# A feed-forward part that starts under the end of an attention part: the first norms of the last two batches, the second batch's bias step and the first activation are put in other places

## The reference, cut to what matters

```
x = x + attention(norm(x), ctx)          # 16 heads, softmax
x = x + ffn(norm(x))                     # the part of this change
x = x + mlstm(norm(x), ctx)              # 8 heads, gates, one junction over all batches
x = x + moe_lora(norm(x))

ffn:  h = layernorm(x) * ln1_g + ln1_b
      h = bitlinear(h, w1, b1)           # 256 -> 1024, activations rounded to 8 bits, weights ternary
      h = gelu(h)
      h = layernorm(h) * ln2_g + ln2_b
      h = bitlinear(h, w2, b2)           # 1024 -> 256
```

## Time and profile before

| | us |
|---|---|
| median of three runs | 413.37 |
| lowest, highest | 410.84, 414.47 |
| the profiled execution | 413.97 |
| its span in the profile | 412.3 |
| busy in the span: PE, DVE, ACT, POOL | 334.4, 305.8, 264.3, 183.8 |

### The profile page before, as it was taken

The page is one execution under the profiler, slowest core; times in us unless marked ns, Lnnn a source line. Parts: engine busy times, 40 slices in busy tenths (PEclk is TensorE's granted clock), DMA queues, the critical chain, the costliest instruction groups (busy, mean ns, idle before and its releaser), DMA issues.

```text
span 412.3 us, 9147 instructions
## 1 busy us (share of the span) xinstructions
PE 334.4 (81%) x3086; PEld 236.6 (57%) x3093; DVE 305.8 (74%) x1025; ACT 264.3 (64%) x567; POOL 183.8 (45%) x207
## 2 busy tenths in 40 slices
PE   2989789998999999724667778779488999999774
PEld 1777567776777767402445545456265666666431
DVE  2799736877889888676998999984447877788641
ACT  1466445476455455626789889876578888888520
POOL 1213401122122564239998989962015455544520
PEclk9999999999999999955999999989689999999966
DMA  7799998979634510000000000000002122212000
GB/s 239 211 291 264 262 249 221 234 177 227 134 85 115 123 22 2 1 0 0 2 1 2 0 2 1 2 0 2 0 14 40 40 41 53 52 46 46 16 25 25
DMA packets 43869, 33.68 MB, mean 82 GB/s; under 512 B 19888, under 2 KB 39728, under 8 KB 43696
## 3 DMA queue, kind: packets, MB, share of 16 engines
q1 hardware_dynamic: 43824, 33.11, 32.7%
HBM read 24.71 MB, written 8.39 MB: 80 GB/s over the span
## 4 chain that ended last, share of the span: by engine, by line
PE 57%; DVE 18%; issue 13%; ACT 8%; POOL 3%; DMA 1%; SPq 0%; DVEq 0%; ACTq 0%; POOLq 0%
PE PS L1461 6%; PE PS L1157 5%; PE PS L1238 5%; PE PS L1227 4%; DVE sm L741 4%; PE PS L1296 4%; PE PS L1218 4%; PE PS L1217 4%; PE PS L1451 4%; PE PS L1257 3%; PE PS L1446 3%; PE PS L1424 3%; ACT pT L991 2%; DVE sm L713 2%; PE PS L1400 2%
## 5 line engine op out<-in xcount | busy, mean ns | idle before, releaser
L991 ACT ACTIVATE pT<-PS 128x512 f32<-128x512 f32 x64 | 36.5, 596 | 48.2 <-PE PS L1218 47.9
L606 DVE TENSOR_REDUCE negm<-PS 128x4 bf16<-128x512 f32 x64 | 42.3, 684 | 13.0 <-PE PS L1227 12.8
L435 POOL TENSOR_TENSOR sm<-sm,mhalf 128x1 f32<-128x1 f32 x16 | 11.3, 708 | 81.1 <-DVE sm L638 81.1
L451 POOL TENSOR_TENSOR kst<-kst,rows 128x1024 f32<-128x1024 f32 x16 | 37.7, 2354 | 6.4 <-ACT kst L1059 6.3
L1103 ACT ACTIVATE lnT<-PS,Atok 128x128 f32<-128x128 f32 x128 | 36.5, 369 | 4.3 <-PE PS L1402 2.7
L1336 PE MATMUL PS<-identf,w2f 128*128 128x128 f32 x128 | 19.2, 298 | 21.0 <-ACT w2f L1048 20.8
L1218 PE MATMUL PS<-identb,negm 128*128 128x128 bf16 x256 | 34.9, 220 | 0.0
L465 POOL TENSOR_TENSOR kst<-kst,rows 128x1024 f32<-128x1024 f32 x14 | 33.1, 2366 | 0.0
L1238 PE MATMUL PS<-pT,vx 128*32 128x128 f32 x512 | 27.0, 285 | 5.2 <-ACT pT L991 5.2
L1336 PEld LDWEIGHTS PS<-identf,w2f 128*128 128x128 f32 x128 | 15.1, 151 | 25.5 <-ACT w2f L1048 20.2
L1461 PE MATMUL PS<-wd,xT 128*128 128x392 f32 x64 | 28.0, 565 | 1.8 <-DVE rest L885 1.8
(11 more groups left out here) (220 smaller groups left out, 975.6 us busy)
## 6 DMA issues: line engine op xcount, KB each, us to landing
scr_q<-qpart SPq DMA_DIRECT2D x8, 384.0 KB, 3.4
scr_k<-kpart SPq DMA_DIRECT2D x8, 384.0 KB, 4.5
X<-in_x SPq DMA_DIRECT2D x8, 256.0 KB, 4.6
CTXT<-in_ctxT SPq DMA_DIRECT2D x8, 256.0 KB, 4.8
vx<-in_ctx SPq DMA_DIRECT2D x16, 128.0 KB, 3.1
out<-rest SPq DMA_DIRECT2D x16, 128.0 KB, 1.7
rows<-in_rows SPq DMA_DIRECT2D x1, 1544.0 KB, 8.4
qst<-scr_q SPq DMA_DIRECT2D x8, 192.0 KB, 4.5
```

What stands on the lines that cost most here:

```text
L451: gp.tensor_tensor(n2[q.slot], n2[q.slot], ln2g, ALU.mult).then_inc(b_g2, 1)
L606: v.tensor_reduce(negm[f.slot % 2][:, 4 * hg:4 * hg + 4], PS[:, 2 + hg % 2, :].rearrange("p (h k) -> p h k", h=4), AX_X, ALU.max, negate=T ...
L991: s.activation(pT[:, hg, :], PS[:, hg % 2, :], ACT.Exp, scale=float(DH0) ** -0.5).then_inc(a_e, 1)
```

## The change

- GpSimd: the power (`spread1`) and the bias add (`residual`) of the first norm get functions of their own. For batch 14 the power stands inside turn 3, between the gain of batch 0 and the scale and shift, and the bias add behind turn 4; for batch 15 the power stands behind turn 4 and the bias add behind turn 6. Turn 2 comes ahead of them all.
- VectorE: the bias step of batch 1 stands ahead of the last residual update and of the first norm of batch 14, no longer in turn 2. Of batch 14, statistics and centring stand ahead of turn 2 and the scaling in turn 3, behind the bias step. Of batch 15, statistics and centring are in turn 4 and the scaling in turn 5. The two memsets of `mv23` stand ahead of the last `normalise`.
- ScalarE: the table set with gelu is asked for right behind the last exponential. In turn 2 the norm of batch 0 stands ahead of the gelu of batch 1. The roundings of batches 14 and 15 stand behind turns 4 and 6.
- TensorE: the transposes of batch 2 stand in the last attention turn, behind the transposes of batch 15's y.

```diff
--- before.py
+++ after.py
@@ -428,14 +428,19 @@
                 pool.wait_ge(s_wq, 3)
                 gp.tensor_scalar(row, row, by, None, ALU.mult).then_inc(s_sr, 1)
 
+            def spread1(d):
+                z = sm1[d.slot % 2]
+                pool.wait_ge(l_w, d.b + 1)
+                gp.tensor_tensor(z[:, 3:4], z[:, 2:3], mhalf[:, 0:1], ALU.pow).then_inc(l_r, 1)
+
+            def residual(d):
+                pool.wait_ge(l_c, d.b * 7 + 4)
+                gp.tensor_tensor(X[:, d.b, :], X[:, d.b, :], b2r, ALU.add).then_inc(l_xb, 1)
+
             def turn_a(_f, _b, _c, d):
                 if d:
-                    z = sm1[d.slot % 2]
-                    pool.wait_ge(l_w, d.b + 1)
-                    gp.tensor_tensor(z[:, 3:4], z[:, 2:3], mhalf[:, 0:1], ALU.pow).then_inc(l_r, 1)
-
-                    pool.wait_ge(l_c, d.b * 7 + 4)
-                    gp.tensor_tensor(X[:, d.b, :], X[:, d.b, :], b2r, ALU.add).then_inc(l_xb, 1)
+                    spread1(d)
+                    residual(d)
                     if 9 <= d.b < 12:
                         scale_rows(d.b - 9)
 
@@ -449,6 +454,9 @@
                         pool.wait_ge(s_sr, 3)
                     pool.wait_ge(b_n2, q.b + 1)
                     gp.tensor_tensor(n2[q.slot], n2[q.slot], ln2g, ALU.mult).then_inc(b_g2, 1)
+
+                if tau == 3:
+                    spread1(Turn(NB - 2, 2, 3))
                 if p or e:
                     now, was = tau % 2, (tau - 1) % 2
                     pool.wait_ge(b_ve, tau - 1)
@@ -465,11 +473,13 @@
                     gp.tensor_tensor(n2[q.slot], n2[q.slot], ln2b, ALU.add).then_inc(b_h2, 1)
 
             turn_a(*peeled(NB, NB, 4, 4))
-            turn_b(2, *peeled(2, NB, 4, 9))
-            turn_a(*peeled(NB + 1, NB, 4, 4))
-            turn_a(*peeled(NB + 2, NB, 4, 4))
-            for tau in range(3, NB + 8):
+            for tau in range(2, NB + 8):
                 turn_b(tau, *peeled(tau, NB, 4, 9))
+                if tau == 4:
+                    residual(Turn(NB - 2, 2, 3))
+                    spread1(Turn(NB - 1, 3, 3))
+                elif tau == 6:
+                    residual(Turn(NB - 1, 3, 3))
 
 
             def turn_cd(_n, _a, b, c, _e, _d):
@@ -752,8 +762,15 @@
                     biased(q)
                     if q.b == NB - 1:
                         scale2(q)
-                if b:
+                if b and b.b > 1:
                     hidden(b)
+
+                if tau == 3:
+                    ln1_scale(before_last, centred[0])
+                elif tau == 4:
+                    centred.append(ln1_centre(last, ln1_stats(last)))
+                elif tau == 5:
+                    ln1_scale(last, centred[1])
                 if d:
                     q4.start(d)
                     zd = sm4[d.slot % 2]
@@ -779,18 +796,16 @@
 
 
             first, last, before_last = Turn(0, 0, 0), Turn(NB - 1, 3, 3), Turn(NB - 2, 2, 3)
-            normalise(last)
             for i in range(2):
                 v.memset(mv23[i][:], 1.0).then_inc(b_mv, 1)
+            normalise(last)
             dve.wait_ge(b_mv, 2)
             stats2(first, 1)
             spreads(first, None, 1)
-            ln1_scale(before_last, ln1_centre(before_last, ln1_stats(before_last)))
+            hidden(Turn(1, 1, 0))
             update(last)
-            centred = ln1_centre(last, ln1_stats(last))
-            turn_b(2, *peeled(2, NB, 4, 9))
-            ln1_scale(last, centred)
-            for tau in range(3, NB + 8):
+            centred = [ln1_centre(before_last, ln1_stats(before_last))]
+            for tau in range(2, NB + 8):
                 turn_b(tau, *peeled(tau, NB, 4, 9))
 
 
@@ -1003,6 +1018,9 @@
                     s.activation(yT2[:].rearrange("p c t -> p (c t)"), PS[:, 7, 0:256], ACT.Copy).then_inc(a_yT2, 1)
                 if b:
                     exp(3)
+                    if b.b == NB - 1:
+
+                        s.preload_act_table_set("gelu_and_others")
                     act.wait_ge(a_pv, b.b * 4 + 4)
                     done(act, a_t4, b, 0)
                     s.activation(yT[:], PS[:, 5, :], ACT.Copy).then_inc(a_yT, 1)
@@ -1024,6 +1042,13 @@
 
                 done(act, b_n2, b, -1)
                 s.activation(gl[b.slot], hb[b.slot], ACT.Gelu, scale=wmean[:, 0:1]).then_inc(b_gl, 1)
+
+            def normed(p, tau):
+                act.wait_ge(b_sh, tau - 1)
+
+                done(act, b_u2, p, -1)
+                s.activation(n2[p.slot], gl[p.slot], ACT.Identity, scale=rs23[tau % 2][:, 0:1],
+                             bias=sh23[tau % 2][:, 0:1]).then_inc(b_n2, 1)
 
             def turn_b(tau, a, b, p, _q, c, d, e, f, g):
                 if d:
@@ -1050,14 +1075,12 @@
                     act.wait_ge(b_t3, f.b + 1)
                     s.activation(QT[:, :, f.b * S:(f.b + 1) * S], PS[:, 7, 0:256].rearrange("p (c t) -> p c t", c=KC),
                                  ACT.Copy).then_inc(b_QT, 1)
+                if p and p.b == 0:
+                    normed(p, tau)
                 if b:
                     gelu(b)
-                if p:
-                    act.wait_ge(b_sh, tau - 1)
-
-                    done(act, b_u2, p, -1)
-                    s.activation(n2[p.slot], gl[p.slot], ACT.Identity, scale=rs23[tau % 2][:, 0:1],
-                                 bias=sh23[tau % 2][:, 0:1]).then_inc(b_n2, 1)
+                if p and p.b > 0:
+                    normed(p, tau)
                 if e:
                     act.wait_ge(b_sh, tau - 1)
                     done(act, b_t3, e, 0)
@@ -1068,12 +1091,12 @@
             columns(Turn(1, 1, 0))
             gelu(Turn(0, 0, 0))
             turn_a(*peeled(NB + 1, NB, 4, 5))
-            turn_b(2, *peeled(2, NB, 4, 9))
-            turn_a(*peeled(NB + 2, NB, 4, 5))
-            turn_b(3, *peeled(3, NB, 4, 9))
-            turn_a(*peeled(NB + 3, NB, 4, 5))
-            for tau in range(4, NB + 8):
+            for tau in range(2, NB + 8):
                 turn_b(tau, *peeled(tau, NB, 4, 9))
+                if tau == 4:
+                    turn_a(*peeled(NB + 2, NB, 4, 5))
+                elif tau == 6:
+                    turn_a(*peeled(NB + 3, NB, 4, 5))
 
 
             act.wait_ge(g_tp, 1)
@@ -1274,6 +1297,8 @@
                     for i in range(KC):
                         last = t.transpose(PS[:, 7, i * 128:(i + 1) * 128], yb[:, i * 128:(i + 1) * 128], identf[:])
                     last.then_inc(a_t2, 1)
+                    if c.b == NB - 1:
+                        columns(Turn(2, 2, 0))
                 if b:
                     pv(0)
                 if f:
@@ -1306,7 +1331,7 @@
                 return t.transpose(PS[:, 7, 256 + b * 16:256 + (b + 1) * 16], PRET[:, b * S:(b + 1) * S], identf[0:16, 0:16])
 
             def turn_b(a, _b, _p, _q, c, d, _e, f, _g):
-                if a:
+                if a and a.b > 2:
                     columns(a)
                 if f:
                     if f.b == 0:
```

## The result

Over 20 runs each, the changed kernel takes a median of 411.31 us (408.02 to 414.12), the kernel before 413.91 (410.84 to 417.37): a ratio of 0.9939, 95% interval 0.9919 to 0.9958. That is 2.6 us faster, where 6.2 were forecast; 411.31 lies above the top of the range, 410.8.

A forecast was written before the change was run, and what follows sets the result against it. The prediction took the attention to feed-forward hand-over (GpSimd queue, table load, gelu waits) as the bound. A lead of 6.35 us, counted as 6.2, gave 407.8 off the profiled 413.97 and 407.2 off the median; it took 407.5, range 404.8 to 410.8.

The forecast's parts named there:

- The hand-over: Attention to feed-forward: waits for GpSimd, table load and gelus bound it; a lead won there travels to the end.
- The table load: ScalarE: moved from the first gelu to behind the last exponential, it starts that gelu 1.3 us earlier.
- VectorE's idle in turn 2: Turn 2, norm of batch 0 ahead of the second gelu: VectorE idles 0.8 us before the stats of batch 1.
- the shade of turns 3 to 5: VectorE: batch 14's scaling and batch 15's centring hide behind gelus in turns 3, 4; batch 15's scaling adds 1.24 in turn 5.
- What GpSimd gets in return: GpSimd, turns 3 to 6: extra powers and adds are covered by about 1 us; contention at most 0.47 each, nothing taken.
- forecast lead of 6.35: Hidden step of batch 5 (turn 6) at 197.39 instead of 203.74; 6.2 us of it counted.
- the sum: Stage times added from the hand-over to the hidden step of batch 5, giving 6.35 us earlier, 6.2 counted.
- C: Rival: GpSimd bounds turns 3 to 6, extra work and contention exceeding cover by at most 2 us; 409.5; chance 0.08.
- B: Rival: table load not saved, second load or delayed copies, 1.3 us lost; 408.8 to 409.1; chance 0.07.
- D: Rival: TensorE stays at the lower clock through feed-forward turns, 2 us a turn; slower, up to 419.5; chance 0.05.
- A: Rival: clock dips in drain and junction hit or miss transposes, about 1.6 us each; 405.5 or 410; chance 0.20.
- The doubt about the norm-first order: ScalarE, turn 2: norming batch 0 first costs the second gelu 1.1 us, but GpSimd gets batch 0 at 175.7, not 184.6.

The follow-up runs named there:

- e1: Changed kernel with the centred row (t1) of batches 14 and 15 in PSUM, so the scaling reads one SBUF tensor; 407.97 us, ratio 0.9853 to the kernel before.
- e2: Changed kernel, operands still in SBUF; GpSimd's offset steps in turns 3 and 5 wait for VectorE's scaling; 408.16 us, ratio 0.9862 to the kernel before.
- e7: e1 plus GpSimd's offset step of turn 4 waiting for VectorE's centring of batch 15; 407.74 us, ratio 0.9845 to the kernel before.
- p1: e1 plus an unused VectorE 128x256 add of two SBUF tensors in each of turns 8 to 15; 417.95 us, one run.
- p2: e1 plus an unused VectorE 128x256 add of one PSUM and one SBUF input in each of turns 8 to 15; 408.6 us, one run.
- p3: e1 plus an unused VectorE 128x256 multiplication by a constant, SBUF to SBUF, in each of turns 8 to 15; 415.25 us, one run.
- e4: Changed kernel with the gelu of batch 1 ahead of the norm of batch 0 again; 411.35 us, ratio 0.9927 to the kernel before.
- e5: e1 with the gelu of batch 1 ahead of the norm of batch 0; 410.15 us, ratio 0.9894 to the kernel before.
- e6: Kernel before with only the table load moved behind the last exponential; 412.49 us, ratio 0.9964 to the kernel before.

## Why the prediction was wrong

**The hand-over, as forecast.** What bounded it, and what unlocks it, was read rightly. Distances from the hidden step of batch 0, forecast and measured: of batch 1, 4.89 and 4.85; of batch 2, 10.33 and 10.16. The table load was worth 1.33 to 1.35 for my 1.3. VectorE's idle in turn 2 was 0.75 for my 0.8.

**The step that failed** is the shade of turns 3 to 5, with the sentences under "What GpSimd gets in return". I had the sign of the contention on the wrong engine and its size as a share: "GpSimd also loses time to every bias step that is moved", bounded by 0.47 each, "I take nothing for the end". It is VectorE that waits when it comes second, and it waits for all that is left of a 2.35 us step. From hidden step to hidden step, turn 3 took 7.97 for my 5.91, turn 4 6.22 for 5.91, turn 5 8.64 for 7.02: 3.99 together, less the 0.17 that turn 2 did better. That is 3.82 of the forecast lead of 6.35, and leaves 2.53. The three long records are 2.07, 0.41 and 1.67 over their length, 4.15 in all, 0.16 more than the turns grew by.

Evidence: e1 takes the second SBUF input away and e2 the overlap, and each gives back most of it (2.92 and 2.46). With e7 the distance is 29.66, 0.49 above the 29.17 of my steps (VectorE waited 0.50 for GpSimd's delayed step), a lead of 5.86 for my 6.35. So the sum was nearly right for a kernel in which those steps do not meet. That e7's time is 6.2 us below before, the very number forecast, is in part luck, since the distance gives 5.86 of it.

**What the rows had shown.** L462 took 0.33 beside L641 and 0.19 alone. That was the small end: L641 had started first, so GpSimd waited, and L641 is short. I read a price per VectorE instruction, where the row only showed one order of the two. The moved steps have the other order, a 0.47 step behind a 2.35 one. At the hand-over of before, every scaling had run with GpSimd idle or waiting for it; those rows did not show the case. The last part of the same trace did. There L878 multiplies two SBUF tensors; fourteen of its sixteen records are 0.41 or 0.42 long, and the two that begin behind a GpSimd step take 0.64 and 0.83:

```profile
316.06 0.64 DVE L878 TENSOR_TENSOR hd<-hd,rr 128x256 f32<-128x256 f32 x1
```

```profile
315.74 0.68 POOL L479 TENSOR_TENSOR hd<-yc,rows 128x256 f32<-128x256 f32 x1
```

It ends 0.28 after GpSimd's step, as the long records of the changed kernel do. The other order stands there too: L462 at 271.18 took 0.57 for 0.19 and ended 0.05 after VectorE's L735, which has two SBUF inputs and had begun first. Whoever compares the longest with the shortest record of one line finds both. With them the range had to reach up by the length of what stands beside each moved step, three steps times 2.35 us.

The Trainium skill ("SBUF — State Buffer", Who interferes with whom) states this: VectorE with two SBUF inputs and a GpSimd instruction that reads SBUF take turns, and the second waits for the first to end. I had weighed only the page that names the contention without its size. The runs agree, e1 and p1 against p2 above all. The same section counts VectorE's scalar operations with them, where they run in a two-port mode; p3 agrees (0.83 to 2.28 for 0.29). It makes no exception for narrow steps, but beside GpSimd's power of two columns in e4 the scaling did not wait (0.48), and there the measurement decides.

**The rivals.** C had the right engine pair and the wrong mechanism: GpSimd's own cover held (in turns 3 to 7 it waited 0.21 to 1.42 us for ScalarE's norm before each gain step), and VectorE never waited for L473 in turns 5 to 7. B did not happen: one load, at 167.06. D did not: TensorE fell to the lower level twice, and eight transposes took 1.97 at 202.08,

```profile
202.08 1.97 PE L1361 MATMUL PS<-identf,w2f 128*128 128x128 f32 x8 [4.20 <-ACT w2f L1073]
```

but the turn around them, 200.76 to 206.72, took its 5.96. A happened in part: the block of transposes in the drain that had taken 1.97 now ran at the upper level,

```profile
268.70 1.09 PE L1361 MATMUL PS<-identf,w2f 128*128 128x128 f32 x8 [1.18 <-ACT w2f L1073]
```

but from the hidden step of batch 5 to the tanh only 0.23 us were won, so my 1.6 for such a dip was too much. e4 shows that this block is not what the tanh waits for: there it took 1.97 again (at 269.05), and the same stretch took 85.54 us, against 85.53 in the changed kernel. What A got right is that executions differ by some 2 us with the clock behind the tanh; the change itself moved that part by 0.39.

**The doubt about the norm-first order** was settled as small: 0.2 us at the hidden step of batch 3 (e1 against e5).

## What to carry to other kernels

A VectorE instruction that reads two SBUF tensors, or a scalar one from SBUF to SBUF over hundreds of columns, must not be placed where a long GpSimd step may already run: its price there is what is left of that step, not a share of its own length, and a gap that looks idle on VectorE's list is no shade for it. Put one operand into PSUM, or let GpSimd wait for the short VectorE step first. Look in the trace of before for lines whose longest record is far above their shortest. When work is moved, list for each moved instruction what runs on the neighbour engine at the new place, and bound the cost by that instruction's length.

## What the runs showed of the hardware

- VectorE, 128x256 fp32, beside a GpSimd step of 1024 columns: 0.48 us with one of two inputs in PSUM (0.41 for a plain add), 0.96 to 2.55 with both in SBUF, ending 0.27 to 0.29 us after GpSimd's record each time. Since the instruction needs 0.47, it seems to start some 0.2 before that record's end; the profile is rough on GpSimd.
- The reverse order: GpSimd's L462 took 0.57 for 0.19 behind a VectorE instruction with two SBUF inputs (before, 271.18), and its bias add 0.91 for 0.72 (e1, 187.06).
- Two rows do not fit a wait to the end. In e4 the scaling took 0.48 beside GpSimd's power of two columns (179.75, 0.71 us). In before, a VectorE scalar step of 256 columns (L595, 155.41) took 1.09 for 0.29 beside a GpSimd scalar step of 2.98 (155.11), and ended 1.6 ahead of its end. No run looked into either.
- One SBUF input and an SBUF output is no protection by itself: p3's scalar form waited like the others. The hidden step (PSUM and an SBUF row, SBUF output) took 1.27 or 1.28 in every trace. VectorE's largest magnitude over 1024 columns, with one SBUF input, took its 1.21 inside GpSimd's wide steps (before, 268.80).
- The table switch cost 1.28 us, and no second term shows in front of the next instruction, which begins 0.02 behind it (changed kernel, 168.36): moved alone, it gave 1.35 (e6).
- TensorE's granted clock in the first feed-forward turns does not matter here: in the changed kernel it was 0.51 from 178 to 192 and 0.50 from 199 to 205, and VectorE's list has no wait for TensorE in either stretch.
